# Causal attention with a rotary embedding: scores three query blocks ahead, and both rotation products taken from PSUM

## The chip, the core and the metric

The kernel runs on one core of one Trainium2 chip. A core has a matrix engine (TensorE, PE in the profile), three elementwise engines (VectorE or DVE, ScalarE or ACT, GpSimd or POOL) and a sync engine (SP) that here only issues DMAs. PE reads SBUF and writes PSUM, which has eight banks of 512 float32 columns on 128 partitions. Each engine works through its own list of instructions in order and waits on semaphores for the others. The metric is the device time of one execution in microseconds.

## The reference, cut to what matters

One post-norm transformer layer on x of shape (4, 1024, 128), in float32: attention with 8 heads of width 128 and a causal mask, then a gated feed-forward part of four layers. The attention is

```python
q = rope(einsum('btm,mhd->bthd', x, w_aq)); k = rope(einsum('btm,mhd->bthd', x, w_ak))
v = einsum('btm,mhd->bthd', x, w_av)
s = einsum('bihd,bjhd->bhij', q, k) / 128 - 1e30 * (i < j)
r = einsum('bhij,bjhd,hdm->bim', softmax(s), v, w_ao)
x = layernorm(x + r); x = layernorm(x + ffn(x))
# rope: [even*cos - odd*sin, even*sin + odd*cos], even and odd being the two halves of the 128 columns
```

## The kernel before, in words

There are 32 heads (4 batches of 8), run one after the other in 16 pairs, an even and an odd head each. A head has 8 query blocks of 128 rows; block ib sees ib + 1 key blocks. Every product of Q, K, V and of the probabilities is made of three matmuls, since each float32 operand is split in a high and a low part. V and the output projection are one matrix per head, so the V projection of a pair stands in the even head alone (V_STEP, `project_v`).

Each engine runs the same function `step(head, s, b)` for s = 0 to 7 of every head, with its own work in it. What stands in which step is what sets the order of the kernel; there is no scheduler. In step s:

- PE issues the scores of a block ahead of s (`scores`, L391 to L395), the transposes of the probabilities of block s (`transpose_probs`, L404), the projections of Q and K for the next head (`project_qk`, four tiles of 512 columns, QK_STEP), V, and pieces of probabilities times V (`attend`; chunk 0 in steps 6 and 7, chunk 1 in steps 1 to 3 of the next head).
- DVE takes the negated maximum of a row of scores (`negative_max`, L629), the inverse of the row sum (`inverse_sum`, L635), and the low part of the transposed probabilities (`transposed_low`, L645).
- ACT takes the exponential out of PSUM into one of four `probs` buffers (`exponentiate`, L525), with the row sum as a by-product, and the high part of the transposed probabilities (`transposed_high`, L537).
- POOL multiplies the probabilities by the inverse sum (`normalize`, L720).

The scores of a block lie in PSUM banks 0 and 1 when ib is even and 2 and 3 when it is odd. `wait_for_banks` makes PE wait for whoever read a bank last: for scores it is the exponential of two blocks before, for a transpose or a projection `t_low` or `cos_done`. So the scores of block 1 wait for the exponential of block 7 of the head before.

The rotation of one tile goes through a chain: projected by PE, copied to `proj` by ACT (`copy_projected`, L548), the halves swapped by two DMAs from SP into `swapped`, times the sine on POOL (`times_sin`, L725), times the cosine from PSUM on DVE (`times_cos`, L653), the sum on DVE (`rope_sum`, L660), its high part on ACT (`roped_high`, L556), its low part on POOL (`roped_low`, L732). Tables at the top say in which step each happens, a value of 8 being step 0 of the following head. The scores of blocks 0 to 3 wait for the low part of tile 1, those of blocks 4 to 7 for that of tile 3.

Before the first head the same steps run without scores; DVE there also makes the low parts of x of the other batches (`low_of_x`, L604) in step 5, ahead of the first maximum. The feed-forward part begins when the attention has ended, and has its own lists.

## Time and profile before

| what | value |
|---|---|
| three runs | 1076.83, 1079.12, 1079.99 us; median 1079.12 |
| the profiled execution | 1077.77 us, of it 1076.0 us span |
| busy: PE, weight loads of PE | 995.9 us (93%), 859.3 us (80%) |
| busy: DVE, ACT, POOL | 852.0 us (79%), 655.7 us (61%), 584.5 us (54%) |
| granted clock of PE, mean | 0.979 |
| attention, up to the last add into rT, which starts at 784.52 us | 0 to 785 us |
| feed-forward part | 785 to 1076 us |

The span is what the profiler saw from the first to the last instruction; the other 1.8 us of that execution lie around it. Busy shares are means over both parts of the program. In the attention part PE has 3% idle, in the feed-forward part it is again PE that is busy nearly throughout, and none of the changed code runs there. The times under "busy" for PE count overlapping matmuls once.

### The profile page before, as it was taken

The page shows a single profiled execution, that of the slowest core. Times are in us where ns is not written, and L with a number is a line of the kernel's source. Part 1 is how long each engine was busy: PE and PEld are TensorE (multiplying, and loading weights), DVE is VectorE, ACT ScalarE, POOL GpSimd, SP SyncE. Part 2 cuts the span into 40 slices and gives each one's busy share as a digit, 9 for nine tenths or more (in the row PEclk, how much of TensorE's full clock was granted, in tenths as well). Part 3 has the DMA queues.
Part 4 walks back from the last instruction along what each step waited for, and adds up shares of the span by engine and source line. Part 5 has one row for each costly group of instructions (what it writes and reads, how often), then busy time and mean ns, then how long its engine had stood idle before and what let it go on. Part 6 is the DMA issues. An engine that isn't in the chain of part 4 may idle for free. (4 is left out here: it accounts for less than half of the span.)

```text
span 1076.0 us, 20027 instructions
## 1 busy us (share of the span) xinstructions
PE 995.9 (93%) x5648; PEld 859.3 (80%) x5648; DVE 852.0 (79%) x1803; ACT 655.7 (61%) x1383; POOL 584.5 (54%) x536
## 2 busy tenths in 40 slices
PE   2799999999999999999999999999839999999995
PEld 1588888888888888888888888888728878788784
DVE  4888888988889898888888888888755668486744
ACT  4577676777767677777767777777625252343531
POOL 3777777777777877767787777777350101000000
PEclk8799999999999999999999999999969999999998
DMA  7542223432223223232222222221020000000000
GB/s 249 167 137 60 69 61 88 153 89 59 60 69 73 63 58 91 58 77 64 76 49 58 60 60 70 69 68 40 1 79 1 1 1 21 0 19 0 1 20 20
DMA packets 33292, 66.16 MB, mean 61 GB/s; under 512 B 5456, under 2 KB 6992, under 8 KB 32208
## 3 DMA queue, kind: packets, MB, share of 16 engines
q1 hardware_dynamic: 30400, 58.62, 20.6%
q10 hardware_dynamic: 2832, 6.82, 1.7%
q8 instruction: 29, 0.48, 0.2%
q14 instruction: 31, 0.25, 0.1%
HBM read 24.26 MB, written 7.34 MB: 29 GB/s over the span
## 5 line engine op out<-in xcount | busy, mean ns | idle before, releaser
L720 POOL TENSOR_SCALAR probs<-probs,inv_sum 128x128 f32<-128x128 f32 (+7 forms) x256 | 236.7, 925 | 173.5 <-DVE inv_sum L635 173.5
L537 ACT ACTIVATE pT<-psum 128x512 fp32r<-128x512 f32 (+3 forms) x384 | 176.0, 490 | 131.2 <-PE psum L404 130.1
L311 PE MATMUL psum<-pT,vals 128*128 128x512 f32 (+3 forms) x1152 | 242.2, 350 | 1.6 <-DVE rT L678 1.6
L525 ACT ACTIVATE probs<-psum,neg_max 128x128 f32<-128x128 f32 (+7 forms) x256 | 190.3, 744 | 48.8 <-DVE neg_max L629 46.9
L645 DVE TENSOR_TENSOR pT<-psum,pT 128x512 fp32r<-128x512 f32 (+3 forms) x384 | 199.8, 547 | 14.8 <-ACT pT L537 11.8
L311 PEld LDWEIGHTS psum<-pT,vals 128*128 128x128 f32 x1152 | 187.3, 189 | 24.0 <-DVE pT L645 1.7
L629 DVE TENSOR_REDUCE neg_max<-psum 128x1 f32<-128x128 f32 (+7 forms) x256 | 190.4, 744 | 3.7 <-PE psum L395 3.7
L404 PE MATMUL psum<-ident,probs 128*128 128x128 f32 x1152 | 174.6, 276 | 12.8 <-POOL probs L720 6.4
L725 POOL TENSOR_TENSOR swapped<-swapped,rope 128x512 f32<-128x512 f32 x128 | 165.4, 1292 | 37.2 <-DMA swapped<-proj 37.1
L901 PE MATMUL ps<-hid,w 128*128 128x512 f32 x768 | 181.3, 396 | 0.0
L901 PEld LDWEIGHTS ps<-hid,w 128*128 128x128 f32 x768 | 143.8, 188 | 34.4
L732 POOL TENSOR_TENSOR qk<-swapped,qk 128x512 fp32r<-128x512 f32 x128 | 166.1, 1297 | 2.8 <-ACT qk L556 2.8
L404 PEld LDWEIGHTS psum<-ident,probs 128*128 128x128 f32 x1152 | 134.6, 141 | 38.8 <-DVE pT L645 12.4
L391 PE MATMUL psum<-qk 128*128 128x384 f32 (+5 forms) x384 | 136.9, 356 | 25.6 <-POOL qk L732 22.7
L660 DVE TENSOR_TENSOR swapped<-by_cos,swapped 128x512 f32<-128x512 f32 x128 | 122.7, 959 | 41.6 <-POOL swapped L725 41.6
L394 PE MATMUL psum<-qk 128*128 128x384 f32 (+5 forms) x384 | 143.3, 373 | 0.0
L395 PE MATMUL psum<-qk 128*128 128x384 f32 (+5 forms) x384 | 132.0, 344 | 0.0
L311 PE MATMUL psum<-x_moving,w_stage 128*128 128x512 f32 (+1 forms) x384 | 107.0, 415 | 9.9 <-DVEq L622 9.9
L995 ACT ACTIVATE value<-ps,scales 128x512 f32<-128x512 f32 x64 | 43.4, 688 | 97.1 <-PE ps L901 96.5
L391 PEld LDWEIGHTS psum<-qk 128*128 128x128 f32 x384 | 73.0, 190 | 35.7 <-issue 26.5
L1026 POOL COPY y<-y_norm 128x512 f32<-128x512 f32 (+1 forms) x8 | 5.2, 652 | 166.7 <-DVE y_norm L1083 166.7
L548 ACT ACTIVATE proj<-psum 128x512 f32<-128x512 f32 x128 | 75.1, 599 | 31.7 <-PE psum L311 26.3
(78 smaller groups left out, 1267.9 us busy)
## 6 DMA issues: line engine op xcount, KB each, us to landing
swapped<-proj SPq DMA_DIRECT2D x256, 128.0 KB, 2.3
w_stage<-qk_split SPq DMA_DIRECT2D x30, 256.0 KB, 2.6
wv_stage<-v_split SPq DMA_DIRECT2D x15, 256.0 KB, 2.6
x_split<-ffn_raw ACTq DMA_DIRECT2D x2, 1024.0 KB, 5.9
ffn_raw<-g SPq DMA_DIRECT2D x2, 1024.0 KB, 8.1
x_moving<-x_split SPq DMA_DIRECT2D x2, 1024.0 KB, 5.9
out<-y SPq DMA_DIRECT2D x4, 512.0 KB, 2.6
raw_x<-xT SPq DMA_DIRECT2D x3, 512.0 KB, 11.5
```

The lines of the kernel that those rows point to most:

```text
L311: ins = nc.tensor.matmul(out_ap, left[a], right[b], start=first and i == 0, stop=last and i == 2)
L391: nc.tensor.matmul(dst, left[0], right[0], start=True, stop=False)
L394: nc.tensor.matmul(dst, left[0], right[1], start=False, stop=False)
L404: last = nc.tensor.transpose(bank("t", head[1], nth)[:, (jb % 4) * P:(jb % 4 + 1) * P], probs[:, ib % 4, jb * P:(jb + 1) * P], ident[:])
L525: nc.scalar.activation(probs[:, ib % 4, :width].rearrange("p (h c) -> p h c", h=halves), score_ps[:, ib % 2, :halves, :half], ACT.Exp, bia ...
L537: nc.scalar.activation(pT[chunk][:, 0, 4 * f:4 * f + n_blocks, (ib % 4) * P:(ib % 4 + 1) * P], bank("t", head[1], nth)[:, :n_blocks * P].r ...
L629: nc.vector.tensor_reduce(neg_max[:, n:n + 1], score_ps[:, ib % 2, :halves, :half], AX.XY, ALU.max, negate=True).then_inc(max_ready[0], 1)
L645: nc.vector.tensor_tensor(low, bank("t", head[1], nth)[:, :n_blocks * P].rearrange("p (j i) -> p j i", i=P), high.bitcast(F32), ALU.subtra ...
L720: nc.gpsimd.tensor_scalar(p, p, inv_sum[:, n:n + 1], 1.0, ALU.mult, ALU.mult).then_inc(probs_ready[0], 1)
L725: nc.gpsimd.tensor_tensor(swapped[:, j], swapped[:, j], rope[:, 1, c * BANK:(c + 1) * BANK], ALU.mult).then_inc(sin_done[0], 1)
L732: nc.gpsimd.tensor_tensor(low, swapped[:, j], high.bitcast(F32), ALU.subtract).then_inc(rope_low[0], 1)
L901: last = nc.tensor.matmul(ps[:, c, o], w_at(base, a, k * HID, o * P), hid[:, c, layer, b, k], start=k == 0 and i == 0, stop=k == HT - 1 an ...
```

## The change

Three things are done together.

1. LOOK = 3: PE issues the scores of block s + 3 in step s (before, s + 2), DVE the maximum of s + 3, ACT the exponential of s + 2 (before, s + 1), DVE the inverse sum of s + 2, behind the maximum and no longer ahead of it. POOL still normalizes block s + 1 in step s, and PE still transposes block s.
2. The rotation has no copy on ACT. DVE multiplies the projection in PSUM by the sine (`by_sin`) and by the cosine (`by_cos`), the DMAs swap the halves of the sine product, and POOL adds the two. The sign in the sine table is exchanged between the halves for that. On DVE the sum goes, on POOL the product with the sine goes and the sum comes.
3. The tables: projections of the four tiles in steps 7 (of the head before), 0, 2 and 3, where they were in 0, 0, 2, 2; sums on POOL in 1, 2, 4, 6; high and low parts in 2, 3, 5, 7, where they were in 3, 4, 6, 8. The lent banks follow one step earlier.

```diff
-QK_STEP = (0, 0, 2, 2)
-COS_STEP = (0, 0, 2, 2)
-SIN_STEP = (1, 2, 3, 4)
-SUM_STEP = (2, 3, 4, 6)
-HIGH_STEP = (3, 4, 6, 8)
-LOW_STEP = (3, 4, 6, 8)
+LOOK = 3
+QK_STEP = (-1, 0, 2, 3)
+SUM_STEP = (1, 2, 4, 6)
+HIGH_STEP = (2, 3, 5, 7)
+LOW_STEP = (2, 3, 5, 7)
...
-LEND1 = (6, 7, 0)
-LEND3 = (1, 2)
+LEND1 = (5, 6, 7)
+LEND3 = (0, 1)
...
@@ sync
-                        wait_for(sp, proj_copied, head, j)
+                        wait_for(sp, sin_done, head, j)
...
@@ tensor, step
-                    scores(ahead, (s + 2) % NI)
+                    scores(ahead, (s + LOOK) % NI)
...
@@ scalar
-            def copy_projected(head, j):
-                wait_for(act, qk_projected, head, j)
-                old_head, old = earlier(head, j, 2, 4)
-                wait_for_swap(act, old_head, old)
-                wait_for(act, rope_low, step_on(head, -1), j)
-
-                nc.scalar.activation(proj[:, j % 2], bank("qk", 1 if parity(head) else 2, j),
-                                     ACT.Copy).then_inc(proj_copied[0], 1)
...
-                    exponentiate(ahead, (s + 1) % NI)
+                    exponentiate(ahead, (s + LOOK - 1) % NI)
...
@@ vector
+            def rope_products(head, j):
                 c = ROPE_TILES[j][1]
+                projected = bank(*qk_use(head, j))
+                old_head, old = earlier(head, j, 2, 4)
+                wait_for(dve, qk_projected, head, j)
+                wait_for_swap(dve, old_head, old)
+                wait_for(dve, rope_low, step_on(head, -1), j)
+                nc.vector.tensor_tensor(by_sin[:, j % 2], projected, rope[:, 1, c * BANK:(c + 1) * BANK],
+                                        ALU.mult).then_inc(sin_done[0], 1)
+                nc.vector.tensor_tensor(by_cos[:, j], projected, rope[:, 0, c * BANK:(c + 1) * BANK],
                                         ALU.mult).then_inc(cos_done[0], 1)
...
-            def rope_sum(head, j):
-                wait_for(dve, sin_done, head, j)
-                wait_for(dve, cos_done, head, j)
-                nc.vector.tensor_tensor(swapped[:, j], by_cos[:, j], swapped[:, j], ALU.add).then_inc(rope_done[0], 1)
...
@@ gpsimd
-                nc.gpsimd.tensor_tensor(swapped[:, j], swapped[:, j], rope[:, 1, c * BANK:(c + 1) * BANK],
-                                        ALU.mult).then_inc(sin_done[0], 1)
+            def rope_sum(head, j):
                 wait_for_swap(pool, head, j)
+                wait_for(pool, cos_done, head, j)
+                nc.gpsimd.tensor_tensor(swapped[:, j], by_cos[:, j], swapped[:, j], ALU.add).then_inc(rope_done[0], 1)
```

On PE, at the end of the first odd head before, from the last matmul of the scores of block 7 (128x512) on; `128x128 x6` on `probs` are the transposes of block 5, and the 128x128 and 128x256 score matmuls are blocks 0 and 1 of the next head:

```order
L395 MATMUL psum<-qk 128x512
L404 MATMUL psum<-ident,probs 128x128 x6
L391 MATMUL psum<-qk 128x128
L393 MATMUL psum<-mask_r,ident_r 128x128
L394 MATMUL psum<-qk 128x128
L395 MATMUL psum<-qk 128x128
L404 MATMUL psum<-ident,probs 128x128 x7
L311 MATMUL psum<-pT,vals 128x512 x3
L311 MATMUL psum<-pT,vals 128x384 x3
L391 MATMUL psum<-qk 128x256
```

The same place in the changed kernel, where the transposes are those of blocks 4 and 5:

```order
L400 MATMUL psum<-qk 128x512
L409 MATMUL psum<-ident,probs 128x128 x5
L396 MATMUL psum<-qk 128x128
L398 MATMUL psum<-mask_r,ident_r 128x128
L399 MATMUL psum<-qk 128x128
L400 MATMUL psum<-qk 128x128
L409 MATMUL psum<-ident,probs 128x128 x6
L396 MATMUL psum<-qk 128x256
```

The scores of block 7 now come a step earlier, and between them and the scores of block 1 there are 5 + 6 transposes and block 0; before there were 6 + 7 transposes, block 0 and six matmuls of probabilities times V.

On DVE, before the first head, from the last rotation sum of tile 0 to the first maximum (`neg_max`), before:

```order
L660 TENSOR_TENSOR swapped<-by_cos,swapped 128x512
L653 TENSOR_TENSOR by_cos<-psum,rope 128x512 x2
L683 TENSOR_TENSOR v_parts<-psum,v_parts 128x1024
L685 CAST ident_r<-ident 128x128
L686 CAST mask_r<-mask_f 128x128
L660 TENSOR_TENSOR swapped<-by_cos,swapped 128x512 x2
L604 TENSOR_TENSOR x_moving<-raw_x,x_moving 128x1024
L604 TENSOR_TENSOR ffn_raw<-raw_x,ffn_raw 128x1024 x2
L660 TENSOR_TENSOR swapped<-by_cos,swapped 128x512
L629 TENSOR_REDUCE neg_max<-psum 128x1
```

and in the changed kernel, from the cosine product of tile 2 on:

```order
L652 TENSOR_TENSOR by_cos<-psum,rope 128x512
L676 TENSOR_TENSOR v_parts<-psum,v_parts 128x1024
L678 CAST ident_r<-ident 128x128
L679 CAST mask_r<-mask_f 128x128
L650 TENSOR_TENSOR by_sin<-psum,rope 128x512
L652 TENSOR_TENSOR by_cos<-psum,rope 128x512
L598 TENSOR_TENSOR x_moving<-raw_x,x_moving 128x1024
L598 TENSOR_TENSOR ffn_raw<-raw_x,ffn_raw 128x1024 x2
L623 TENSOR_REDUCE neg_max<-psum 128x1 x2
```

The three kinds of sums in between are gone, and the low parts of x (L604, now L598) stand directly behind the products of tile 3.

On POOL, from the normalization of block 6 of the first head on, before:

```order
L720 TENSOR_SCALAR probs<-probs,inv_sum 128x896
L720 TENSOR_SCALAR probs<-probs,inv_sum 128x1024
L732 TENSOR_TENSOR qk<-swapped,qk 128x512
L720 TENSOR_SCALAR probs<-probs,inv_sum 128x128
L720 TENSOR_SCALAR probs<-probs,inv_sum 128x256
```

and in the changed kernel, from block 5 on:

```order
L711 TENSOR_SCALAR probs<-probs,inv_sum 128x768
L716 TENSOR_TENSOR swapped<-by_cos,swapped 128x512
L711 TENSOR_SCALAR probs<-probs,inv_sum 128x896
L722 TENSOR_TENSOR qk<-swapped,qk 128x512
L711 TENSOR_SCALAR probs<-probs,inv_sum 128x1024
L716 TENSOR_TENSOR swapped<-by_cos,swapped 128x512
L711 TENSOR_SCALAR probs<-probs,inv_sum 128x128
L722 TENSOR_TENSOR qk<-swapped,qk 128x512
```

The sum of tile 3 now stands between the normalizations of blocks 7 and 0, and the low part of tile 3 ahead of block 1.

## Rows read from the trace of the kernel before

**Rows 1.** Windows of the trace; columns: stretch, length, busy time of each engine, clock, DMA.

```profile
0.00:40.00 40.00, 14.74 (x56) 11.93 (x57) 21.82 (x29) 16.73 (x29) 16.31 (x17) 0.79 0.74 252
40.00:780.00 740.00, 715.20 (x4420) 633.33 (x4419) 642.62 (x1262) 531.58 (x1198) 545.85 (x502) 1.00 0.27 70
```

**Rows 2.** The waits of PE between 40 and 780 us.

```profile
PE psum L391 <- POOL qk L732: 10.2, 15, 0.7
PE psum L404 <- POOL probs L720: 6.4, 19, 1.0
PE psum L404 <- DVE pT L645: 6.1, 17, 1.4
```

**Rows 3.** Timeline of PE: first score matmuls of two even heads (start, duration, engine).

```profile
76.74 0.33 PE L391 MATMUL psum<-qk 128*128 128x128 f32 x1 [0.62 <-POOL qk L732]
...
729.36 0.32 PE L391 MATMUL psum<-qk 128*128 128x128 f32 x1 [0.70 <-POOL qk L732]
```

**Rows 4.** Timeline of PE, end of an odd head.

```profile
400.90 0.39 PE L395 MATMUL psum<-qk 128*128 128x512 f32 x1
401.13 0.60 PE L404 MATMUL psum<-ident,probs 128*128 128x128 f32 x4
401.98 0.44 PE L404 MATMUL psum<-ident,probs 128*128 128x128 f32 x2 [0.25 <-DVE pT L645]
403.12 0.32 PE L391 MATMUL psum<-qk 128*128 128x128 f32 x1 [0.70 <-POOL qk L732]
...
404.04 0.98 PE L404 MATMUL psum<-ident,probs 128*128 128x128 f32 x7 [0.26 <-POOL probs L720]
```

**Rows 5.** Timeline of DVE and ACT at the same place, query block 7.

```profile
402.12 1.20 DVE L629 TENSOR_REDUCE neg_max<-psum 128x1 f32<-128x1024 f32 x1
...
403.35 1.11 ACT L525 ACTIVATE probs<-psum,neg_max 128x1024 f32<-128x1024 f32 x1 [0.51 <-DVE neg_max L629]
```

**Rows 6.** Timeline of PE, end of an even head.

```profile
421.58 0.71 PE L404 MATMUL psum<-ident,probs 128*128 128x128 f32 x5
422.05 0.95 PE L311 MATMUL psum<-wv_stage,x_moving 128*128 128x256 f32 x6
...
424.41 0.85 PE L404 MATMUL psum<-ident,probs 128*128 128x128 f32 x6
425.11 0.98 PE L311 MATMUL psum<-wv_stage,x_moving 128*128 128x256 f32 x6
425.93 0.22 PE L391 MATMUL psum<-qk 128*128 128x128 f32 x1
...
426.41 0.83 PE L404 MATMUL psum<-ident,probs 128*128 128x128 f32 x5
```

**Rows 7.** Groups by line, all engines; last numbers: busy us, mean ns, idle before.

```profile
L645 DVE TENSOR_TENSOR pT<-psum,pT 128x512 fp32r<-128x512 f32 (+3 forms) x384 | 199.8, 547 | 14.8 <-ACT pT L537 11.8
...
L537 ACT ACTIVATE pT<-psum 128x512 fp32r<-128x512 f32 (+3 forms) x384 | 176.0, 490 | 131.2 <-PE psum L404 130.1
...
L725 POOL TENSOR_TENSOR swapped<-swapped,rope 128x512 f32<-128x512 f32 x128 | 165.4, 1292 | 37.2 <-DMA swapped<-proj 37.1
...
L660 DVE TENSOR_TENSOR swapped<-by_cos,swapped 128x512 f32<-128x512 f32 x128 | 122.7, 959 | 41.6 <-POOL swapped L725 41.6
...
L653 DVE TENSOR_TENSOR by_cos<-psum,rope 128x512 f32<-128x512 f32 x128 | 83.2, 684 | 6.6 <-ACT proj L548 4.5 <-DMA ident<-ident_in 1.1
```

**Rows 8.** Timeline of all engines, the fill before the first head.

```profile
18.36 2.48 POOL L725 TENSOR_TENSOR swapped<-swapped,rope 128x512 f32<-128x512 f32 x2 [14.07 <-DMA swapped<-proj]
...
28.16 3.20 DVE L604 TENSOR_TENSOR ffn_raw<-raw_x,ffn_raw 128x1024 fp32r<-128x1024 f32 x2
...
32.95 0.28 DVE L629 TENSOR_REDUCE neg_max<-psum 128x1 f32<-128x128 f32 x1
...
33.60 0.19 ACT L525 ACTIVATION_READ_ACCUMULATOR probs<-psum,neg_max 128x1 f32 x1
...
33.94 0.66 PE L391 MATMUL psum<-qk 128*128 128x384 f32 x1 [2.61 <-ACT probs L525]
```

More of the change, by code:

```diff
@@ L65 @@
 NQK, NV = len(QK_STEP), len(V_STEP)
+QK_AHEAD = [1 - step // NI for step in QK_STEP]
 PV_BANK = 7
@@ L77, in plan_banks @@
         for s in range(NI):
-            ib, tile_off = (s + 2) % NI, off + (s + 2) // NI
+            ib, tile_off = (s + LOOK) % NI, off + (s + LOOK) // NI
             first = 2 * (ib % 2)
@@ L82, in plan_banks @@
             after = ([("t", off, FIRST_FILL[s] + k) for k in range(FILLS_OF[s])]
-                     + [("qk", off + 1, j) for j in range(NQK) if QK_STEP[j] == s]
+                     + [("qk", off + QK_AHEAD[j], j) for j in range(NQK) if QK_STEP[j] % NI == s]
                      + [("v", 0, c) for c in range(NV) if V_STEP[c] == NI * off + s])
@@ L132, in attention @@
     qk = sb("qk", [P, 2, 2, 2, T], F32R)
-    proj = sb("proj", [P, 2, BANK])
+    by_sin = sb("by_sin", [P, 2, BANK])
     by_cos = sb("by_cos", [P, NQK, BANK])
@@ L242, in run_pairs @@
     def run_pairs(eng, body):
+        body((-1, 0), NI - 1, 0)
         for s in range(NI):
@@ L277, in before_first @@
     def before_first(head):
-        return isinstance(head[0], int) and head[0] < 0
+        return isinstance(head[0], int) and number(head) == -1
     def pair_exists(pair):
@@ L285, in bank, with qk_use @@
         return psum[:, USES[use][0] * BANK:(USES[use][0] + 1) * BANK]
+    def qk_use(head, j):
+        off = (parity(head) - QK_AHEAD[j]) % 2
+        return "qk", off + QK_AHEAD[j], j
     def wait_for_banks(pe, pair, *use):
@@ L408, in project_qk @@
             def project_qk(running, nth):
-                head = step_on(running, 1)
+                head = step_on(running, QK_AHEAD[nth])
                 if nth == 0:
@@ L454, in step @@
             def step(head, s, b):
-                ahead = step_on(head, (s + 2) // NI)
+                ahead = step_on(head, (s + LOOK) // NI)
                 if before_first(head) and s == 1:
@@ L463, in step @@
                     last.then_inc(vo_ready, 1)
-                if before_first(head) and s == NI - 2:
+                if before_first(head) and s == NI - LOOK:
                     pe.wait_ge(masks_ready, 1)
@@ L471, in step @@
                 for target, j in rope_tasks(head, s, QK_STEP):
-                    project_qk(step_on(target, -1), j)
+                    project_qk(head, j)
                 for c in v_tasks(head, s):
@@ L566, in step @@
             def step(head, s, b):
-                ahead = step_on(head, (s + 1) // NI)
+                ahead = step_on(head, (s + LOOK - 1) // NI)
                 if before_first(head) and s == 1:
@@ L573, in step @@
                         high_of_x(b)
-                if before_first(head) and s == NI - 2:
+                if before_first(head) and s == NI - LOOK:
                     save_weights()
-                if before_first(head) and s == NI - 1:
+                if before_first(head) and s == NI - LOOK + 1:
                     act.wait_ge(vo_low, 1)
@@ L591, in step @@
                     transposed_high(head, s)
-                for target, j in rope_tasks(head, s, QK_STEP):
-                    copy_projected(target, j)
                 for c in v_tasks(head, s):
@@ L689, in step @@
                         low_of_x(b)
[L690 to L695 removed]
+                if exists(step_on(head, (s + LOOK) // NI)):
+                    negative_max(step_on(head, (s + LOOK) // NI), (s + LOOK) % NI)
+                if exists(step_on(head, (s + LOOK - 1) // NI)):
+                    inverse_sum(step_on(head, (s + LOOK - 1) // NI), (s + LOOK - 1) % NI)
                 if s == ADD0_STEP:
@@ L701, in step @@
                     transposed_low(head, s)
-                for target, j in rope_tasks(head, s, COS_STEP):
-                    times_cos(target, j)
+                for target, j in rope_tasks(head, s, QK_STEP):
+                    rope_products(target, j)
                 for c in v_tasks(head, s):
@@ L737, in step @@
                     normalize(ahead, (s + 1) % NI)
-                for target, j in rope_tasks(head, s, SIN_STEP):
-                    times_sin(target, j)
+                for target, j in rope_tasks(head, s, SUM_STEP):
+                    rope_sum(target, j)
                 for target, j in rope_tasks(head, s, LOW_STEP):
```

18 lines of the change are left out of this document (2 added, 16 removed).

## The prediction, made before the changed kernel was run

> **What bounds the kernel now.** I read the busy shares by window first, then the waits of PE, then the timeline around the longest of them. PE is busy 715.20 of the 740.00 us between 40 and 780 us; DVE with 642.62 us, ACT with 531.58 and POOL with 545.85 are all under 87% [rows 1]. So PE sets the time of the attention, and what can be won there is what it stands still: 740.00 - 715.20 = 24.8 us. Three kinds of waits hold most of it: for the low part of the rotation on POOL (10.2 us in 15 waits), for normalized probabilities (6.4 us) and for the low part of transposed probabilities (6.1 us) [rows 2]. The 15 waits are one per pair of heads: 14 pairs take 729.36 - 76.74 = 652.6 us, 46.6 us each, and both even heads in these rows begin with that wait [rows 3]. The other part that the change touches is the fill, where PE is busy 14.74 of 40 us [rows 1]. The feed-forward part is not touched.
>
> The idle time of the rows is a little less than what the waits cost, since matmuls overlap. I take the starts instead. At the end of an odd head four transposes take 401.98 - 401.13 = 0.85 us, where five take 0.47 in an even head; the two behind them take 403.12 - 401.98 = 1.14 us, where 0.2 would do by that rate; block 0 takes 404.04 - 403.12 = 0.92 us against 0.48 [rows 4, 6]. That is 0.4 + 0.9 + 0.4 = 1.7 us, and the even head adds some 0.1, so about 1.8 us per pair is lost, all of it in steps 5 and 6.
>
> **What the change takes away.** In step s PE needs the normalized block s, and POOL gets it a step earlier relative to its inverse sum. Steps 5 and 6 take POOL out of PE's way there: the 6.4 us go. The low part of tile 1 is due in step 3 and needed in step 5, the same two steps as before, but POOL ran late only because it waited for inverse sums; without that I take the 10.2 us as gone too, and the 6.1 us, since DVE is relieved: 128 sums of 0.959 us go, 128 products of 0.684 us come, 122.7 - 87.6 = 35 us of its 852 [rows 7]. ACT loses 128 copies; it was never waited for. On POOL the sum stands for the product, at 1.292 us each [rows 7], so it gains and loses nothing. All this work lies beside PE. It takes off the whole 1.8 us per pair, and nothing more.
>
> The 0.959 us deserves a look: it is the mean of an instruction with two inputs in SBUF, where the product with one input in PSUM has 0.684 [rows 7]. The Trainium skill, SBUF — State Buffer, section "Who interferes with whom", says that a VectorE instruction with two SBUF inputs contends with GpSimd's reads and one with a single SBUF input does not; the trace agrees. Its page Perfetto Trace Analysis, section "Optimizing Scalar/DVE Operations", speaks against such a change, since work moved between these two engines may gain nothing through the shared port. By that rule POOL's adds would be slowed by DVE's products; by the row of the product that reads PSUM they are not, and neither is in the sum, because DVE is not what PE waits for after it.
>
> **What the change adds: a new wait of PE, at the scores of block 1.** They use the PSUM banks of block 7 of the head before, so they wait for its exponential. Before, this was two steps later with 13 transposes, block 0 and six matmuls between. Now block 7 is in step 4 and block 1 in step 6, with 11 transposes and block 0 between in an odd head. Call E the end of the scores of block 7 (401.29 us in the row, 400.90 + 0.39). PE's next start is at E - 0.16 [rows 4]. Five transposes 0.47 us, block 0 0.48, six transposes 0.70 [rows 6]: PE is at block 1 at E + 1.5. The exponential is not there: the maximum of 1024 columns takes 1.20 us, the exponential starts 0.03 later and takes 1.11 [rows 5], the read of its sum ends some 0.1 later, and PE starts 0.15 us behind that read (33.60 + 0.19 to 33.94 [rows 8]). With 0.04 for the first hand-over that is E + 2.6. **The new wait is 1.1 us in every odd head.** Nothing hides it: behind it in PE's list stand the transposes of block 6 and probabilities times V, which could run but have to queue. In an even head two groups of V projections lie between, 0.82 us each by 425.93 - 425.11 [rows 6], which brings PE to E + 3.1; but ACT has one more copy ahead of the exponential (0.49 us is the mean of its copies [rows 7], a full bank takes a little more), so it comes at about E + 3.3. I take 0.2 us there.
>
> A second place is behind it, in steps 6 to 1. POOL has, from the end of that exponential (E + 2.5) on, the low part of tile 2 (behind ACT's high part, 0.6), the normalization of block 7 and the sum of tile 3, three operations of 1.3 us: E + 7.0. ACT then makes the high part of tile 3 ahead of the two transposed high parts of block 7: three of 0.5 to 0.6 us, E + 8.7. DVE follows with the second low part, 0.55, and the products of tile 0, two of 0.68: E + 10.6, and only then takes the maximum of block 3, half of the 1.20 us of block 7, then ACT its exponential, half of 1.11 with the read, then PE: E + 12.0 [rows 5, 7]. That exponential frees the bank for block 5. PE gets there after four of eight steps: half of 46.6 / 2 = 23.3 us is 11.7, less the V projections (four groups of 0.82, half of it per head, 1.6), so E + 2.6 + 10 = 12.6. It comes out close, so I add 0.1 us per pair and keep 0 and 0.8 as bounds.
>
> Sum per pair: -1.8 + 1.1 + 0.2 + 0.1 = -0.4 us; for 15 pairs -6 us. The bounds: from -1.8 us (if the new wait were covered), -27 us, to +0.3 (the second place at its upper end), +5 us.
>
> **The fill.** Before, DVE gets to the first maximum at 32.95 us, behind a rotation sum and the low parts of x, which end at 31.36 (28.16 + 3.20); the exponential's read ends at 33.79 and from 33.94 us PE runs almost without a break [rows 8]. POOL started at 18.36 us, when the first swaps had landed [rows 8]. Now DVE waits for the same swap before the products of tile 2 (its buffer is reused), at about 17.5 to 18.4: products 1.4, low part of the V weights 1.2, the two casts 2.1, products of tile 3 1.4, low parts of x 3.2 + 1.2. From 17.5 that is 28.0, from 18.4 28.9, and the maximum follows at once. The durations are those of the operations in the trace: a [128, 512] product is 0.684 us [rows 7] and two low parts of x are 3.20 [rows 8]; the rest I estimate at that rate per column. So the first maximum moves from 32.95 to 28 to 29 us: -5 us, bounds -2 and -6. The swap is issued later by the wait for the sine table, but in both kernels it lies behind the loads of x. Everything behind it moves with it, the rise of PE's clock included, which comes only when PE has begun to run steadily.
>
> At the end of the last head the scores are a step earlier but the chain from the last exponential to the last product is as long: 0.
>
> **Sum.** 1077.77 - 6 - 5 = 1066.8 us. The profiled execution is 1.4 us below the median of the runs shown, within their spread of 3.2 us, so I say 1067 us.
>
> **The rivals.**
> A. The new wait at block 1 doesn't show: DVE, relieved of its sums, and ACT would be early enough. For it speaks that before, PE never waited for an exponential in the steady part [rows 2]; against it that 1.20 + 1.11 us are the two operations themselves and no queue. Time: 1077.8 - 5 - 27 = 1046 us. (The Trainium skill, Perfetto Trace Analysis, section "Identifying the Most-Contended Engine", warns that matmul busy time is a poor measure of headroom and takes weight loads instead; those are at 633.33 of 740.00 us [rows 1], so by that rule even more could be won. The stretches of back-to-back matmuls show no such reserve.)
> B. The waits only change their names: the new wait is 1.4 us or more, in both heads, or POOL's low parts still come late, and a pair takes 46.6 us as before. Only the fill is left: 1077.8 - 5 = 1073 us. For it: POOL's list is no shorter.
> C. Slower. The second place decides: if POOL's operations take 1.7 us in place of 1.3 while DVE is busy (the sums on DVE had a mean 40% above the 0.684 us of the product [rows 7]), the chain grows by 3 x 0.4 = 1.2 us on POOL, and by 0.6 more on ACT and DVE, to E + 13.8 against PE's 12.6. That is 1.2 us per pair where I have 0.1, and with POOL's delay carried into the low part of tile 3 another 0.5: 1066.8 + 15 x 1.6 = 1091 us. It decides from 12.6 + 0.75 us on, where it has eaten the fill too. Against it: POOL has 26% idle in that window [rows 1], and V gives even heads 3 us of room.
> D. The change doesn't do what it says, as the fill still waits for the swap at 18.4 and the low parts of x are late by their loads: fill -2 in place of -5, 1070 us.
>
> **How the numbers follow.** Forecast with its own range, 1060 to 1071 us: 0.45. A 0.13, or between it and the forecast: 0.1 more. B 0.15, D 0.06, C 0.11. The range 1050 to 1078 us leaves most of A and C out. What a measurement of this kernel can tell from no change is 0.3%, 3.2 us, so between 1075.9 and 1082.3 us is no change. From the cases: faster 0.84, no change 0.07 (the upper part of B), slower 0.09.
>
> **What would show it.** Right: PE waits for an exponential at the scores of block 1 of 128x256 once per pair, about 1 us, 15 to 17 us in all; the waits for POOL's low part and for normalized probabilities are nearly gone; the first maximum starts at 28 to 29 us; a pair takes 46.2 us; DVE is busy some 35 us less. Wrong: a pair under 45.5 us (A); a wait of PE for an exponential at the scores of blocks 3 to 6, or for POOL, with a pair over 46.6 us (B, C); the first maximum after 31 us (D).

## The result and the profile after

The changed kernel takes **1087.69 us** (median of six runs, 1084.84 to 1089.49), the kernel before 1079.03 us (six runs, 1076.83 to 1081.03) on the same chips. The ratio is 1.008, with a 95% interval of 1.006 to 1.010: it is slower by 0.8%, where 1067 us and a gain were forecast. The profiled execution took 1089.37 us, its span is 1087.6 us against 1076.0.

The page of the changed kernel, engines first, then two of its groups (busy us, mean ns, idle before):

```profile
PE 1000.1 (92%) x5648; PEld 861.6 (79%) x5648; DVE 814.1 (75%) x1803; ACT 586.6 (54%) x1255; POOL 540.1 (50%) x536
...
L711 POOL TENSOR_SCALAR probs<-probs,inv_sum 128x128 f32<-128x128 f32 (+7 forms) x256 | 192.7, 753 | 152.7 <-DVE inv_sum L629 152.5
...
L552 ACT ACTIVATE qk<-swapped 128x512 fp32r<-128x512 f32 x128 | 80.3, 627 | 34.5 <-POOL swapped L716 33.9
```

Three engines have less to do: DVE 38 us, ACT 69 and POOL 44 of busy time less than before. The kernel is slower all the same. The products cost what the forecast had (0.681 us), and so do POOL's sums (1.295). POOL's normalization has even become quicker, 753 ns where it had 925. Idle time has grown in several queues; DVE alone now stands 102.6 us before its maxima, waiting for PE, and that costs nothing by itself. The growth that matters below is ACT's before the high parts of the rotation: 33.9 us waiting for POOL's sum, where it was 3 us waiting for DVE's.

Windows of the changed kernel (columns as in [rows 1]):

```profile
0.00:40.00 40.00, 19.33 (x79) 16.35 (x80) 24.20 (x37) 16.30 (x30) 18.05 (x20) 0.83 0.78 259
40.00:780.00 740.00, 706.32 (x4338) 623.71 (x4337) 594.25 (x1239) 456.13 (x1057) 496.63 (x496) 1.00 0.27 69
```

PE stands still for 33.7 us of the 740, where it was 24.8 [rows 1]. Its waits between 40 and 790 us:

```profile
PE psum L396 <- ACT probs L530: 14.3, 15, 1.0
PE psum L409 <- DVE pT L639: 7.4, 16, 0.5
PE psum L316 <- DVE rT L671: 4.5, 15, 0.4
PE psum L316 <- DMA w_stage<-qk_split: 2.8, 1, 2.8
...
PE psum L409 <- POOL probs L711: 1.5, 1, 1.5
```

The waits of [rows 2] for POOL's low part are gone, and all but one of those for probabilities. The first row is the forecast new wait, once per pair. The three rows under it were not forecast; the second has the name of a row of [rows 2], but its wait stands at another place, in the even heads (below). Pairs of heads begin, to be read beside [rows 3] (timeline of PE, start and duration):

```profile
69.02 0.31 PE L396 MATMUL psum<-qk 128*128 128x128 f32 x1
...
216.00 0.31 PE L396 MATMUL psum<-qk 128*128 128x128 f32 x1
...
738.74 0.31 PE L396 MATMUL psum<-qk 128*128 128x128 f32 x1
```

The fourteen pairs take 669.7 us, 17.1 us more than before. Thirteen of them take 47.5 to 47.6 us each (46.6 before) and one, with heads 6 and 7, takes 52.0 and ends at 216.00. Head 2 begins 7.7 us earlier, of which 3.9 are the fill (below); a step is 2.9 us, so most of the rest can be put down to its scores standing a step earlier in PE's list, which doesn't move the end. So the account of the span is: fill -3.9, fourteen pairs +0.9 each or +12.6, the long pair +4.5 on top, the rest -1.6: together +11.6 us.

**Where a pair loses it.** PE at the end of an odd head and in the first steps of the next (beside [rows 4]):

```profile
501.67 0.84 PE L409 MATMUL psum<-ident,probs 128*128 128x128 f32 x6
503.44 0.38 PE L396 MATMUL psum<-qk 128*128 128x256 f32 x1 [0.93 <-ACT probs L530]
...
509.71 0.27 PE L409 MATMUL psum<-ident,probs 128*128 128x128 f32 x1
510.17 0.98 PE L316 MATMUL psum<-x_moving,w_stage 128*128 128x512 f32 x3 [0.18 <-DVE pT L639]
...
511.98 0.38 PE L409 MATMUL psum<-ident,probs 128*128 128x128 f32 x2
512.62 1.65 PE L316 MATMUL psum<-pT,vals 128*128 128x512 f32 x6 [0.26 <-DVE rT L671]
```

Read the starts. Six transposes take 1.77 us to the next start, 0.70 would do [rows 6]: so 1.07 us are lost to the exponential of block 7. Then there are two places in steps 0 and 1 of the next head: from one transpose to the next start it takes 0.46 us, and from two transposes 0.64, where z1_low6 below, without these waits, has 0.02 and 0.21. That is 0.44 and 0.43 us lost. And PE at the end of an even head (beside [rows 6]):

```profile
525.22 0.62 PE L409 MATMUL psum<-ident,probs 128*128 128x128 f32 x4
526.30 0.44 PE L409 MATMUL psum<-ident,probs 128*128 128x128 f32 x2 [0.46 <-DVE pT L639]
526.50 0.98 PE L316 MATMUL psum<-wv_stage,x_moving 128*128 128x256 f32 x6
...
527.79 1.25 PE L409 MATMUL psum<-ident,probs 128*128 128x128 f32 x7
528.83 0.38 PE L316 MATMUL psum<-wv_stage,x_moving 128*128 128x256 f32 x1
```

The six transposes of block 5 take 1.28 us, where 0.70 would do, and the seven of block 6 take 1.04, where 0.82 would (seven at that rate): 0.58 and 0.22 us lost. The sum is 1.07 + 0.44 + 0.43 + 0.58 + 0.22 = 2.7 us per pair, against the 1.8 us that the change removed: +0.9, which is what the pairs show.

**The chain behind the two places in steps 0 and 1**, all engines in the same stretch:

```profile
505.25 1.15 POOL L711 TENSOR_SCALAR probs<-probs,inv_sum 128x1024 f32<-128x1024 f32 x1
...
506.33 1.30 POOL L716 TENSOR_TENSOR swapped<-by_cos,swapped 128x512 f32<-128x512 f32 x1
...
507.67 0.63 ACT L552 ACTIVATE qk<-swapped 128x512 fp32r<-128x512 f32 x1 [1.29 <-POOL swapped L716]
...
508.21 1.07 ACT L542 ACTIVATE pT<-psum 128x512 fp32r<-128x512 f32 x2
...
508.82 1.29 DVE L639 TENSOR_TENSOR pT<-psum,pT 128x512 fp32r<-128x512 f32 x2 [1.34 <-ACT pT L542]
...
511.89 0.67 DVE L671 TENSOR_TENSOR rT<-psum,rT 128x512 f32<-128x512 f32 x1
```

From top to bottom each row releases the next, directly or as the instruction behind it in its queue. POOL normalizes block 7 and then sums tile 3. ACT waited 1.29 us for that sum, with the high part of the transposed block 7 queued behind it; PE had begun those transposes at 506.65. DVE waited 1.34 us for that high part. The low part of block 7 frees the bank in which PE projects tile 1 (510.17). Behind it DVE has two products of tile 0, a maximum and an inverse sum, and then the add into rT, which frees the bank of probabilities times V (512.62). POOL is late in this chain because the low part of tile 2 stood ahead of both (503.99 to 505.28).

**The one long pair.** The SP queue around 186 us, and windows of the same place:

```profile
185.72 0.92 SPq L374 DMA_DIRECT2D ffn_raw<-f  x2
186.68 0.91 SPq L374 DMA_DIRECT2D ffn_raw<-g  x2
...
188.10 0.43 SPq L357 DMA_DIRECT2D w_stage<-qk_split  x1
```

```profile
190.00:196.00 6.00, 5.89 (x44) 5.29 (x42) 5.02 (x13) 5.03 (x14) 4.98 (x5) 1.00 0.99 373
196.00:202.00 6.00, 3.24 (x13) 2.87 (x13) 2.58 (x4) 1.31 (x4) 0.76 (x2) 0.77 0.08 30
```

The weights of the feed-forward part are issued just ahead of the stage of weights that head 8 is projected from. The DMA engines are 0.99 busy, the stage lands 10.3 us after its issue (2.7 is the median of these loads), and PE, which now projects tile 0 a step earlier, stands 2.76 us. Then the granted clock is lower for a while: 0.53 from 199 to 202 us, near the level of 1.2 GHz, and 1.00 in the three microseconds before.

**The fill** (beside [rows 8]):

```profile
23.41 2.34 DVE L598 TENSOR_TENSOR x_moving<-raw_x,x_moving 128x1024 fp32r<-128x1024 f32 x1
...
29.01 0.61 DVE L623 TENSOR_REDUCE neg_max<-psum 128x1 f32<-128x128 f32 x2
...
30.00 0.66 PE L396 MATMUL psum<-qk 128*128 128x384 f32 x1 [4.38 <-ACT probs L530]
```

The first maximum starts at 29.01 us (32.95 before) and PE goes on at 30.00 (33.94): 3.9 us won. The forecast's 5 us had this first low part of x at 1.2 us, as it was before (1.21). It takes 2.34 here: a sum on POOL starts within 0.01 us of it and lasts 1.27 us, and both read two operands from SBUF.

### The profile page after: what moved, and what is told of

Read it like the earlier page. It is cut to its first block and busy times, and to the rows that moved or that the text cites. A ratio compares the mean times of both kernels' runs of the same rounds, so it can differ in the third digit from the quotient of the medians.

```text
span 1087.6 us, 19704 instructions
## 1 busy us (share of the span) xinstructions
PE 1000.1 (92%) x5648; PEld 861.6 (79%) x5648; DVE 814.1 (75%) x1803; ACT 586.6 (54%) x1255; POOL 540.1 (50%) x536
## 5 line engine op out<-in xcount | busy, mean ns | idle before, releaser
L623 DVE TENSOR_REDUCE neg_max<-psum 128x1 f32<-128x128 f32 (+7 forms) x256 | 192.7, 753 | 102.7 <-PE psum L400 102.6
L711 POOL TENSOR_SCALAR probs<-probs,inv_sum 128x128 f32<-128x128 f32 (+7 forms) x256 | 192.7, 753 | 152.7 <-DVE inv_sum L629 152.5
L316 PE MATMUL psum<-pT,vals 128*128 128x512 f32 (+3 forms) x1152 | 238.5, 347 | 6.1 <-DVE rT L671 6.1
L316 PEld LDWEIGHTS psum<-pT,vals 128*128 128x128 f32 x1152 | 192.4, 189 | 38.8 <-DVE rT L671 5.6
L716 POOL TENSOR_TENSOR swapped<-by_cos,swapped 128x512 f32<-128x512 f32 x128 | 165.8, 1295 | 70.5 <-DMA swapped<-by_sin 70.5
L722 POOL TENSOR_TENSOR qk<-swapped,qk 128x512 fp32r<-128x512 f32 x128 | 165.5, 1293 | 46.2 <-ACT qk L552 46.2
L316 PE MATMUL psum<-x_moving,w_stage 128*128 128x512 f32 (+1 forms) x384 | 123.3, 431 | 15.0 <-DVEq L616 10.0
L552 ACT ACTIVATE qk<-swapped 128x512 fp32r<-128x512 f32 x128 | 80.3, 627 | 34.5 <-POOL swapped L716 33.9
L650 DVE TENSOR_TENSOR by_sin<-psum,rope 128x512 f32<-128x512 f32 x128 | 87.2, 681 | 7.8 <-PE psum L316 3.9
```

What stands on the lines that cost most here:

```text
L316: ins = nc.tensor.matmul(out_ap, left[a], right[b], start=first and i == 0, stop=last and i == 2)
L623: nc.vector.tensor_reduce(neg_max[:, n:n + 1], score_ps[:, ib % 2, :halves, :half], AX.XY, ALU.max, negate=True).then_inc(max_ready[0], 1)
L711: nc.gpsimd.tensor_scalar(p, p, inv_sum[:, n:n + 1], 1.0, ALU.mult, ALU.mult).then_inc(probs_ready[0], 1)
L716: nc.gpsimd.tensor_tensor(swapped[:, j], by_cos[:, j], swapped[:, j], ALU.add).then_inc(rope_done[0], 1)
L722: nc.gpsimd.tensor_tensor(low, swapped[:, j], high.bitcast(F32), ALU.subtract).then_inc(rope_low[0], 1)
```

## The experiments

The theory after the result is that the loss comes from places in the queues, in the look-ahead half and its tables, and not from the rotation half. The rivals: the rotation half causes it (GpSimd's sums, contention between DVE and POOL), or the look-ahead itself does, by the exponential of block 7. Ratios below are to the kernel before, measured beside each kernel, with 95% intervals; "pair" is the usual distance of even heads. The changed kernel has 1.008 and 47.5 us.

### The two halves apart

**r1_rotation**: the new rotation with the scores two blocks ahead and the tables of before; the inverse sum stays behind the maximum, as in the changed kernel.

```diff
+LOOK = 2
 QK_STEP = (0, 0, 2, 2)
+SUM_STEP = (1, 2, 3, 4)
...
-                if exists(step_on(head, (s + 1) // NI)):
-                    inverse_sum(step_on(head, (s + 1) // NI), (s + 1) % NI)
-                for target, j in rope_tasks(head, s, SUM_STEP):
-                    rope_sum(target, j)
...
+                if exists(step_on(head, (s + LOOK - 1) // NI)):
+                    inverse_sum(step_on(head, (s + LOOK - 1) // NI), (s + LOOK - 1) % NI)
```

> The rotation half alone: both products from PSUM on DVE, sum on POOL, but scores two blocks ahead and the step tables of before (projections 0,0,2,2; the POOL sum in 1,2,3,4 where the sine product stood; high and low parts 3,4,6,8). Theory 1 (the look-ahead half made the loss): 1065 to 1079 us, pair of heads 46.0 to 46.6 us, waits of PE for POOL's low part still there. Theory 2 (the rotation half made the loss, through POOL waiting for the swaps): 1085 us or more, pair of heads over 47.2 us.

Measured: 1145.53 us, ratio 1.060 (1.057 to 1.064), pair 51.3 us. It is no clean half. POOL's waits between 220 and 740 us:

```profile
POOL probs L711 <- DVE inv_sum L629: 195.1, 121, 2.7
```

Before it was 115.6 us there. With the scores two ahead, POOL needs the inverse sum in the very step in which DVE makes it, so behind the maximum it is too late. An order that fits three blocks ahead spoils a kernel with two (r3_rotation shows that it is this order). Part of the 6% is the clock: the granted clock is 0.97 between 220 and 740 us, where the changed kernel has 1.00. In the six microseconds from 282 us, behind a wait of PE of 1.59 us for POOL's low part, it is 0.72, and from 333 us, a pair later, again 0.72. The run says nothing of the rotation.

**r3_rotation**: the same with the inverse sum ahead of the maximum, as before.

```diff
+                if exists(step_on(head, (s + LOOK - 1) // NI)):
+                    inverse_sum(step_on(head, (s + LOOK - 1) // NI), (s + LOOK - 1) % NI)
                 if exists(step_on(head, (s + LOOK) // NI)):
                     negative_max(step_on(head, (s + LOOK) // NI), (s + LOOK) % NI)
-                if exists(step_on(head, (s + LOOK - 1) // NI)):
-                    inverse_sum(step_on(head, (s + LOOK - 1) // NI), (s + LOOK - 1) % NI)
```

> The rotation half alone once more, now with DVE's inverse sum ahead of the maximum as before the change (in r1 it stood behind, where it waits for the next scores). Theory 1 (the 66 us of r1 came from that order at two blocks of look-ahead, since POOL waited 195 us in the part from 220 to 740 us for inverse sums; the rotation half itself costs little): 1075 to 1095 us, POOL's wait for inverse sums back at some 115 us. Theory 2 (the sum on POOL behind the swaps is what costs): 1120 us or more.

Measured: 1072.16 us, ratio 0.992 (0.988 to 0.995), below what either theory expected. The rotation half alone is a gain of 0.85%. The pairs show little of it: most take 46.2 us, but some 47 and more, and fourteen take 651.4 us (652.6 before); in the trace 2.2 us come from head 2 beginning earlier. This run and the changed kernel differ in the look-ahead, its tables and the place of the inverse sum alone, so these took the ratio from 0.992 to 1.008.

**r2_look**: three blocks ahead, with the tables of the changed kernel, the rotation of before (POOL's products in steps 0, 1, 3, 5).

```diff
+COS_STEP = (-1, 0, 2, 3)
+SIN_STEP = (0, 1, 3, 5)
...
-                            sp.dma_start(swapped[lo:lo + 64, j], by_sin[hi:hi + 64, j % 2]).then_inc(
+                            sp.dma_start(swapped[lo:lo + 64, j], proj[hi:hi + 64, j % 2]).then_inc(
```

> The look-ahead half alone: scores three blocks ahead and the changed kernel's tables, but the rotation as before (copy on ACT, sine on POOL in steps 0,1,3,5, sum on DVE in 1,2,4,6). Theory 1: slower than before, 1085 to 1100 us, with a wait of PE for an exponential of about 1 us per pair, and the late first projection of head 8. Theory 2: faster than before, 1060 to 1075 us, pair 46.2 us or less.

Measured: 1116.5 us, ratio 1.034 (1.031 to 1.038), pair 48.4 us; between 40 and 790 us PE waits 26.4 us for the low part of transposed probabilities and 18.9 for exponentials. The longer chain of the old rotation doesn't fit the new tables, so 3.4% is not the price of the look-ahead alone. With these tables this half gives no gain, under the old rotation or, by the step from r3_rotation to the changed kernel, under the new one. The two halves also show who slowed POOL's normalization. POOL's group of r2_look and then of r3_rotation:

```profile
L728 POOL TENSOR_SCALAR probs<-probs,inv_sum 128x128 f32<-128x128 f32 (+7 forms) x256 | 241.1, 944 | 59.8 <-DVE inv_sum L643 59.8
```

```profile
L711 POOL TENSOR_SCALAR probs<-probs,inv_sum 128x128 f32<-128x128 f32 (+7 forms) x256 | 192.4, 751 | 216.1 <-DVE inv_sum L629 215.4
```

944 ns with DVE's sums of two SBUF inputs, 751 without them, for the same operation. The shapes taken apart confirm it: in the kernel before, 31 of the 32 normalizations of 512 columns run beside such a sum and none of 896 columns does. They take 1177 and 1013 ns; in the changed kernel it is 697 and 1015.

### The places in the changed kernel, one at a time

**z1_low6**: POOL's low part of tile 2 a step later, and nothing else.

```diff
-LOW_STEP = (2, 3, 5, 7)
+LOW_STEP = (2, 3, 6, 7)
```

> The changed kernel with POOL's low part of tile 2 in step 6 in place of 5, ACT's order untouched. Theory 1 (the chain is POOL's sum of tile 3, then ACT's high part of it, then block 7's high part): the sum of tile 3 starts about 0.6 to 1.3 us earlier, so half or more of the 0.9 us in steps 0 and 1 goes: pair 46.9 to 47.2 us, 1077 to 1083 us. Rival (only ACT's order counts): 1087 us.

Measured: 1075.96 us, ratio 0.995 (0.994 to 0.997), pair 46.65 us. All engines at the place of the chain (the even head starts at 490.28, at 501.19 in the changed kernel):

```profile
495.57 0.63 ACT L552 ACTIVATE qk<-swapped 128x512 fp32r<-128x512 f32 x1
...
498.80 0.27 PE L409 MATMUL psum<-ident,probs 128*128 128x128 f32 x1
498.82 0.95 PE L316 MATMUL psum<-x_moving,w_stage 128*128 128x512 f32 x3
...
500.59 0.38 PE L409 MATMUL psum<-ident,probs 128*128 128x128 f32 x2
500.80 0.50 PE L316 MATMUL psum<-pT,vals 128*128 128x512 f32 x1
```

ACT's high part starts 5.3 us behind the head's start where it was 6.5, and both waits of PE are gone (0.02 and 0.21 us to the next start). One entry of a table is worth 0.85 us per pair, about 12 us in fourteen pairs: it turns the loss into a small gain, more than was expected. This settles the largest part of the loss that the forecast had not seen. The same edit also shortens the wait of head 8 to 1.7 us.

**x2_high**: ACT copies the transposed block ahead of the rotation's high part.

```diff
-                for target, j in rope_tasks(head, s, HIGH_STEP):
-                    roped_high(target, j)
                 if exists(head):
                     transposed_high(head, s)
+                for target, j in rope_tasks(head, s, HIGH_STEP):
+                    roped_high(target, j)
```

> The changed kernel, but ACT makes the transposed high part of a block ahead of the high part of the rotation in each step. Theory 1 (POOL's sum of tile 3 holds ACT, ACT holds the high part of block 7, and so DVE): the waits of PE in step 0 (for the low part of block 7, 0.4 us) and step 1 (for the add of chunk 0, 0.5 us) of the head after an odd one go, about 0.9 us per pair, 1073 to 1078 us. Rival (DVE is late through its own load): 1087 us, both waits stay.

Measured: 1081.35 us, ratio 1.001 (0.999 to 1.003), pair 47.0 us. It won about half of what was expected. The same chain is cut one link further on, and the two waits go here too. But the low part of tile 2 is now later still, and the normalization of block 7 behind it:

```profile
503.07 1.09 PE L409 MATMUL psum<-ident,probs 128*128 128x128 f32 x8 [0.47 <-POOL probs L711]
```

A part is given back, which it isn't where the low part itself is moved.

**x1_add1**: the add of chunk 1 at the end of step 3, out of the way of DVE's low part of block 4 in even heads, which frees the bank for the last two transposes of block 5.

```diff
-ADD0_STEP, ADD1_STEP = 0, 4
+ADD0_STEP, ADD1_STEP = 0, 3
...
-                if s == ADD1_STEP:
-                    add_head(step_on(head, -1), 1)
...
+                if s == ADD1_STEP:
+                    add_head(step_on(head, -1), 1)
```

> The changed kernel, but DVE adds chunk 1 of the head before at the end of step 3 in place of step 4, so that the low part of block 4 is not behind it. Theory 1: PE's wait inside the transposes of block 5 in even heads (0.6 us, for the low part of block 4) goes, and some of the 0.3 us at block 6: 0.6 to 0.9 us per pair, 1074 to 1079 us. Rival (DVE was not late there, the bank is late for another reason): 1087 us and the wait stays.

Measured: 1088.71 us, ratio 1.0065 (1.0043 to 1.0086), pair 47.5 us: nothing. PE in the even head:

```profile
525.21 0.93 PE L409 MATMUL psum<-ident,probs 128*128 128x128 f32 x6
525.90 0.97 PE L316 MATMUL psum<-wv_stage,x_moving 128*128 128x256 f32 x6
...
528.50 0.55 PE L409 MATMUL psum<-ident,probs 128*128 128x128 f32 x3 [0.56 <-DVE pT L639]
528.83 0.39 PE L316 MATMUL psum<-wv_stage,x_moving 128*128 128x256 f32 x1
```

The transposes of block 5 no longer wait (0.69 us to the next start, for 1.28), and 528.83 us is reached at the same hundredth: the wait has moved to the transposes of block 6. Their second group needs a bank that DVE's low part of block 5 frees, and this one waits 0.84 us for ACT's high part. The two even-head waits are one budget, and at its end stands ACT; the add was only the first to show in it.

**x3_ffn**: the loads of feed-forward weights behind the stage for head 8, not ahead of it.

```diff
+                        if isinstance(pair, int) and pair == PAIRS_OF and q == 0:
+                            sp.wait_ge(x_saved, X_SAVED)
+                            for base, part in zip(FFN_AT, ffn_weights):
+                                sp.dma_start(ffn_raw[:, base:base + part.shape[1]], part).then_inc(ffn_loaded, 16)
...
-            sp.wait_ge(x_saved, X_SAVED)
-            for base, src in zip(FFN_AT, ffn_weights):
-                sp.dma_start(ffn_raw[:, base:base + src.shape[1]], src).then_inc(ffn_loaded, 16)
```

> The changed kernel, but SP issues the loads of the feed-forward weights behind the weights of head 8, not ahead of them. The first projection of head 8 stands a step earlier since the change and waited 2.8 us for its weights, with PE's clock falling after it. Theory 1 (one place, once in the run): that wait goes, the pair around it takes 47.5 us like the others in place of 52.0, 4.5 us less in all, 1083 us. Rival (the long pair is something else, such as the loads slowing the swaps): the pair stays over 50 us and the time at 1087 us.

Measured: 1084.84 us, ratio 1.004 (1.003 to 1.005); every pair takes 47.5 to 47.6 us, the long one too. The order of two groups of DMAs was worth 4.5 us in the traces and 4.4 by the ratios.

### Together, and a step too far

**y1_order**: x2_high and z1_low6 together.

```diff
-LOW_STEP = (2, 3, 5, 7)
+LOW_STEP = (2, 3, 6, 7)
```

> The changed kernel with ACT's transposed high part ahead of the rotation's high part, and POOL's low part of tile 2 in step 6 (behind the normalization of block 7 and the sum of tile 3) in place of step 5. Theory 1 (POOL's list in steps 5 and 6 is the second place of the chain): the 0.6 us that the order on ACT alone had lost at the transposes of block 7 goes, and the two waits in steps 0 and 1 stay away; pair 46.2 to 46.5 us, 1068 to 1072 us. Rival (POOL is full there, and any order costs the same): pair 47.0 us, 1080 us.

Measured: 1073.18 us, ratio 0.991 (0.989 to 0.994), pair 46.4 us, 1 us above the range expected. What x2_high gave back is not given back here.

**y2_pv0**: y1_order, with probabilities times V of chunk 0 in steps 5 and 6 of odd heads, between block 0 and the scores of block 1, and the add of x1_add1.

```diff
-PV0_PIECES = {6: range(0, 2), 7: range(2, 4)}
+PV0_PIECES = ({6: range(0, 2), 7: range(2, 4)}, {5: range(0, 2), 6: range(2, 4)})
-ADD0_STEP, ADD1_STEP = 0, 4
+ADD0_STEP, ADD1_STEP = 0, 3
```

> y1, and in odd heads the first pieces of probabilities times V in steps 5 and 6 in place of 6 and 7 (1.3 us of matmuls ahead of the scores of block 1), and the add of chunk 1 at the end of step 3. Theory 1 (the scores of block 1 come too early after those of block 7, and nothing else): the wait for the exponential, 1.0 us per odd head, goes, and the bank wait of even heads shrinks by 0.2 to 0.9; pair 44.8 to 45.3 us, 1048 to 1055 us. Rival (PE only moves its wait to the next release, as the add of chunk 1 alone did): pair above 45.8 us, 1062 us or more.

Measured: 1065.13 us, ratio 0.985 (0.982 to 0.989), pair 45.85 us. These are the numbers of the rival, 10 us above the range of the theory, although the wait for the exponential is gone. The starts of PE, taken below from y3_all, whose pairs are the same, show where the rest went.

**y3_all**: y2_pv0 with the DMA order of x3_ffn.

> y2 with the feed-forward weights behind the weights of head 8, all the mended places together. Theory 1: 4.5 us below y2, 1044 to 1051 us. Rival: 1058 us or more.

Measured: **1060.55 us, ratio 0.981 (0.978 to 0.984)**, pair 45.85 us throughout, the best version of all. It is 4.6 us below y2_pv0, as expected, and so above the range that was set with y2_pv0's own. PE at the place of the new wait:

```profile
481.05 0.84 PE L410 MATMUL psum<-ident,probs 128*128 128x128 f32 x6
481.64 1.47 PE L316 MATMUL psum<-pT,vals 128*128 128x512 f32 x6
482.95 0.28 PE L397 MATMUL psum<-qk 128*128 128x256 f32 x1
```

and all that its list of waits still has between 220 and 740 us:

```profile
PE psum L397 <- POOL qk L723: 2.0, 8, 0.3
```

Six matmuls of probabilities times V now fill the time of the exponential. But this list leaves out much of what is lost, since a late start can hide behind overlapping matmuls. From the scores of block 3 to those of block 4 PE now takes 2.26 us (487.08 to 489.34), where y1_order has 1.67 (498.67 to 500.34): of the 1.07 us won, 0.6 are lost again to the low part of tile 3. And in the even head, from the scores of block 0 to those of block 2:

```profile
502.77 0.22 PE L397 MATMUL psum<-qk 128*128 128x128 f32 x1
...
509.25 0.33 PE L397 MATMUL psum<-qk 128*128 128x384 f32 x1
```

These 6.48 us were 6.47 in y1_order (513.75 to 520.22) and 6.76 in the changed kernel and in z1_low6 (524.82 to 531.58, 512.99 to 519.76). So ACT's order took 0.3 us of the 0.8 lost there, and the moved add took nothing; the rest is still lost, though no wait is listed. With y3_all the deeper look-ahead goes with a gain, once other work is put into the gap that it opens. What it adds by itself is not shown, since no run has these orders with scores two blocks ahead.

**y4_pool7**: y3_all, POOL's low part of tile 3 ahead of the normalization of block 0, for the wait ahead of block 4.

```diff
-                if exists(ahead):
+                if exists(ahead) and s < NI - 1:
                     normalize(ahead, (s + 1) % NI)
...
                     roped_low(target, j)
+                if exists(ahead) and s == NI - 1:
+                    normalize(ahead, (s + 1) % NI)
```

> y3 with POOL's low part of tile 3 ahead of the normalization of block 0 in step 7. y3 still waits 0.36 us per pair ahead of the scores of block 4 for that low part. Theory: it goes, pair 45.5 us, 1055 to 1057 us. Rival (ACT's high part is what is late there, which stands behind block 7's in y3): 1060 us.

Measured: 1092.64 us, ratio 1.011 (1.007 to 1.014), pair 47.8 us. POOL, and PE behind it:

```profile
508.37 1.27 POOL L723 TENSOR_TENSOR qk<-swapped,qk 128x512 fp32r<-128x512 f32 x1 [1.05 <-ACT qk L553]
509.62 0.82 POOL L712 TENSOR_SCALAR probs<-probs,inv_sum 128x128 f32<-128x128 f32 x2
```

```profile
510.13 0.32 PE L410 MATMUL psum<-ident,probs 128*128 128x128 f32 x1 [1.55 <-POOL probs L712]
```

The low part waits for ACT with the short normalization queued behind it, whose inverse sum had long been made, and PE waits for that. It is the fault of the changed kernel once more, made larger: 2 us per pair.

**y5_add0**: y4_pool7, with the add of chunk 0 moved from step 0 to step 7 for odd heads.

```diff
-                if s == ADD0_STEP:
+                if s == ADD0_STEP and parity(head):
                     add_head(step_on(head, -1), 0)
+                if s == NI - 1 and parity(head):
+                    add_head(head, 0)
```

> y4 and the add of chunk 0 of an odd head in its step 7, in place of step 0 of the next. It takes PE's last wait for that add (0.2 us per pair) and 0.7 us of DVE's work out of step 0. Theory: 2 to 4 us below y4, 1051 to 1055 us. Rival (DVE has nothing to spare in step 7 and the low part of block 7 gets later): not faster than y4.

Measured: 1090.84 us, ratio 1.009 (1.005 to 1.012), not to be told from y4_pool7: it stands on that kernel's wait, and so says nothing of the add.

## Why the prediction was wrong

The measured 1087.69 us lies outside the forecast's range of 1060 to 1071 us and outside the wide one of 1050 to 1078; slower had a chance of 0.09.

Right, in its own order: PE bounds the attention. The old waits go, 1.8 us per pair. The new wait is at the scores of block 1, 1.1 us in odd heads (measured 1.07), and y2_pv0 removed it by filling it; none in even heads, where 0.2 was taken. The fill: the first maximum at 28 to 29 us, measured 29.01; it was worth 3.9 us, not 5. The prices of the products and sums held to 1%, and DVE is busy 38 us less for 35.

Wrong, by size:

1. **"A second place is behind it ... so I add 0.1 us per pair and keep 0 and 0.8 as bounds."** This is the step that failed. The chain was named link by link as it runs, POOL's low part of tile 2, normalization of block 7, sum of tile 3, ACT, DVE. But PE was looked for at the scores of block 5, behind the maximum of block 3. The chain reaches that maximum at E + 10.3 (511.23 us, E being 500.89), for E + 10.6 forecast, and no wait follows at block 5. PE pays earlier, at the projection of tile 1, whose bank the low part of block 7 frees, and at the add: 0.44 + 0.43 = 0.87 us, where 0.1 stood and 0.8 was the bound. The forecast followed the chain to its last member and not to the first bank that one of its members held. z1_low6 shows the size by itself: 0.85 us per pair.
2. **"It takes off the whole 1.8 us per pair, and nothing more", with DVE relieved.** The sum of DVE's work fell, but in even heads its low part of block 4 now stands behind the maximum of block 7, of 1.23 us, and an add of 0.67, and ACT's high part of block 5 comes late: 0.58 + 0.22 us that the sum had at nothing. Just before that maximum DVE had stood idle for 1.59 us, waiting for the scores, so having less to do could not help it. Less busy was read as less late.
3. The DMA order at head 8 was not looked at, though the tile that waits for it was known to move a step ahead: 4.5 us once.
4. The fill was worth 3.9 us for 5. The first low part of x took 1.1 us more than before; it ran beside a sum on POOL, which the sum for the fill had at no cost to DVE.

With these sizes the forecast's own sum is -1.8 + 1.07 + 0.87 + 0.80 = +0.94 us per pair for the -0.4 that stood there, 14.1 us for fifteen pairs, and -3.9 + 4.5 for the fill and head 8: 1077.8 + 14.7 = 1092.5 us against 1089.4 for the profiled execution. That is 3 us too much, and what makes up the difference is open.

Of the rivals, C (slower, 1091 us, 0.11) had the sign, the chain and nearly the time, but not its reason: POOL's sums take 1.295 us, not 1.7. Its condition, a delay on POOL carried to PE, was met by the order of the queue, at the speed of before. So its time was right by luck. B and D are out by the rows, and A's condition was met only in y2_pv0, at 1065 us and not 1046, because other waits took its place.

## What to carry to other kernels

When the order in queues is changed, walk the new order from each instruction that waits for another engine to everything queued behind it, and ask of each whose PSUM bank or buffer it frees; the price is paid at the first of these that PE needs, not at the end of the chain. Busy time taken off a side engine need not buy anything: here 151 us less on three engines went with a loss, and one table entry that took one waiting instruction out of the front brought 12 us back. An empty list of waits does not prove that nothing waits: compare the distances between starts of two versions. A tile needed a step earlier also needs its DMA a step earlier: look at what bulk transfer stands ahead of it.

## What the runs showed of the hardware

- A wait of PE can cost more than itself by the clock. In the changed kernel PE stood 2.76 us for a late load; the granted clock, 1.00 before, was 0.53 from 199 to 202 us, near the level of 1.2 GHz, and the pair was 4.5 us longer. In y1_order a wait of 2.9 us came with 0.50 from 196 to 199 us, and the pair took 52.35 us for 46.4. In z1_low6 the wait was 1.7 us, the clock stayed at 1.00, and the pair lost only 1.8. The length of the wait does not decide alone: in r1_rotation a wait of 1.59 us was followed by 0.72 over six microseconds.

- POOL's normalization has a mean of 944 or 925 ns while DVE sums two SBUF operands, and 751 or 753 when DVE's products read one from PSUM, for the same instruction on the same operands. The difference sits in the shapes that run beside such a sum (1177 ns for 697 at 512 columns), and is absent where none does (1013 for 1015 at 896). The Trainium skill, SBUF — State Buffer, section "Who interferes with whom", says that a DVE instruction with two SBUF inputs contends with a GpSimd instruction that reads SBUF, and that one with at most one SBUF input, outside the two-port modes, does not; the trace agrees, with 19% of a group that the change doesn't touch. The Trainium skill, Perfetto Trace Analysis, section "Optimizing Scalar/DVE Operations", says that offloading between the two might not help. Here the sum moved to POOL went with a gain (r3_rotation, 0.992); that run also takes a copy off ACT, so the share of the move is not shown apart.
